# A two-layer state-space network on one core: the second layer's tail in chunks, its gating on GpSimd, and another choice of transposed products

## The chip, the cores and the metric

The kernel runs on one core of one Trainium2 chip. The metric is device time in microseconds (us) of one launch. Engines are named as in the profile: PE is TensorE (PEld its weight loads), DVE is VectorE, ACT is ScalarE, POOL is GpSimd, SP is SyncE, which here only issues DMAs. "PSUM" is the memory that PE writes to; it has 8 banks of 512 columns.

## The reference, cut to what matters

Input x is 16 images of 48 x 48 positions (L = 2304) with 96 channels. Two layers follow each other, and each is a residual state-space block and then a residual quantised feed-forward block:

```
for layer in (0, 1):
    n  = layernorm_over_channels(x)                 # no scale, no bias
    xc, z = split(n @ in_proj_w.T)                  # 192 + 192 channels
    u  = silu(depthwise3x3(xc) + conv_b)
    for k in 4 directions (rows, columns, both reversed):
        dt, B, C = u_k @ x_proj_w[k].T              # 6 + 16 + 16
        delta = softplus(dt @ dt_proj_w[k].T + b)
        h[t] = exp(delta[t]*A) * h[t-1] + delta[t]*u[t]*B[t]   # 192 channels x 16 states
        y_k[t] = sum over 16 states of h[t]*C[t]
    y  = sum of the four y_k, put back in row order, + Ds*u
    layer 0:  y = y*silu(z);  x = x + y @ out_w.T + (conv branch of y, with a squeeze gate)
    layer 1:  y = (y - mean_c y) / sqrt(var_c y + 1e-5) * g + b
              x = x + (y*silu(z)) @ out_w.T
    x = x + quantised_ffn(layernorm(x))             # 96 -> 384 -> 96, float8 and float16 rounding
```

## The kernel before, in words

The 16 images of layer 0 run first, then the 16 of layer 1 (`images`: a hardware loop over 15 images and a last pass of its own). Work is channels on partitions, positions along the free axis. The 192 channels of two directions are packed in three tiles: j = 0 holds channels 0 to 127 of one direction, j = 2 the same of its partner, j = 1 the remaining 64 channels of both. Positions are cut in NC = 3 chunks of CH = 768.

**The scan.** A *block* (`g` in the code, 0 to 17) is one tile and one chunk: ORDER = (1, 2, 0), so blocks 0 to 5 are tile 1, 6 to 11 tile 2, 12 to 17 tile 0. Of each tile's six blocks the first three (p = 0) are directions that run forwards, the other three (p = 1) backwards. A block has 16 *steps* (n), one for each state. In a step ACT makes exp(delta*A) (line 1167), PE brings B to all partitions, DVE does the recurrence as one TENSOR_TENSOR_SCAN over 768 positions (line 1486), POOL multiplies by C (line 1630), which SP has fetched with a DMA, and PE adds the result to a sum in PSUM (`add_state`, line 813) four steps later (LAG = 4). Up to six state buffers (NW) and four of h*C (NH) lie between the engines.

B comes in one of two ways. In a *plain* step PE broadcasts B by two bf16 matmuls (line 801) and DVE multiplies delta*u by it (line 1481) before the scan. In a *turned* step ACT scales the transposed delta*u by B (line 1233, `scale_du`) and PE transposes the product into PSUM (line 781, `turn_product`), so DVE does the scan alone. `TURNED` lists the turned steps by tile, `TURNED_FIRST` those of block 0. Other work is hung on steps by `STEP_AT`: the next block's delta (POOL lines 1649 to 1663, ACT 1133 to 1153), its transposition on PE at step 15 (line 773), z of the input projection in blocks 2 to 5 (line 707), the merge of tile 1's column order in blocks 7 to 9 at step 8 (lines 717, 718), and in `add_state`, for p = 1 blocks, the sums so far and D*u (lines 818, 819, with step 12), and for tile 0 the column-order sum (line 823, with step 14).

**The second layer's tail** (`norm` on PE, ACT and DVE) follows block 17. y lies in `yg` (128 + 64 channels). In order: ACT moves the last chunk's sum out of PSUM (`move_sums`, line 1267) and turns z into silu(z) (`gates`, 1255); PE takes the mean over channels by matmuls with 1/192 (`means`, 1012 and 1014), DVE subtracts it (1572), ACT squares (1318), PE takes the mean of the squares; PE also multiplies silu(z) by the bias part of the weight (`out_proj`, 1021 and 1023: the "shift"); DVE multiplies y by silu(z) (1578); PE projects that; ACT takes the square root (1327), DVE the reciprocal (1584), and DVE scales the projection by it (1590) and adds the shift (1593). PE transposes back to positions on partitions (1030) and DVE adds the residual (1598). All of it is done in two halves of 1152 positions, in PSUM units of 3 banks that are claimed in turn (`claim`, `released`). Between these lie the next image's layer norm on DVE and ACT (`ln_center`, `ln_spread`, `ln_apply`, lines 516 to 541) and its transposition on PE (666).

**The feed-forward part and the front.** The ffn follows in the tail of both layers; next to it DVE and PE do the next image's 3x3 convolution (DVE lines 569 and 572, PE line 691 by diagonal matmuls in four strips), and ACT copies its input (`fill_pad`). ACT then applies silu: `planes` (lines 1091, 1092) to PE's strips, and in `front` line 1060 gives `u[0]`, in row order, and 1061 gives `u[2]`, in column order. Everything of the next image's x_proj (PE 653) waits for them.

Of the kernel before, what the change touches and what calls it, by code (L numbers as in the profile page):

```python
# [82 lines left out]
TURNED = {0: (2, 4, 6, 9, 10, 13, 14, 15), 1: (4, 6, 10, 13, 14), 2: (2, 4, 6, 9, 10, 13, 14, 15)}  # L83
# [52 lines left out]
def columns(layer):  # L136
# [17 lines left out]
    "x_kept": 16, "unit_full": (26, 22),  # L154
# [10 lines left out]
    "z_ready": len(Z_UNITS), "z_copied": len(Z_UNITS), "sz_ready": 2, "merge_ready": NC, "merge_taken": NC, "gated": (0, 4),  # L165
# [3 lines left out]
    "mu_taken": (0, 4), "y_squared": (0, 4), "shift_kept": (0, 2), "ysd_kept": (0, 2), "yrstd_ready": (0, 2), "o_scaled": (0, 2), "o_shifted": (0, 2), "x1_ready": 2,  # L169
# [10 lines left out]
def metaformer(nc, x, wpacks, consts_f, consts_b, mid, c_rows, out):  # L180
    ctx = ExitStack()
    with ctx:
# [398 lines left out]
        U_MU, U_SHIFT, U_VAR, U_SHIFT_1, U_OUT, U_OUT_T = 2, 4, 5, 7, 8, 10  # L581
        U_Q = (16, 12)
# [3 lines left out]
        def _(pe):  # L586
# [8 lines left out]
            def released(k):  # L595
# [13 lines left out]
                for first, end, name, n in [  # L609
                        (U_MU, U_SHIFT, "mu_taken", 2), (U_SHIFT, U_VAR, "shift_kept", 1), (U_VAR, U_SHIFT_1, "ysd_kept", 1),  # L610
                        (U_SHIFT_1, U_OUT, "shift_kept", 2),
                        (U_OUT, U_OUT_T, "o_scaled", 1), (U_OUT_T, q, "x1_ready", 1)]:
                    if first <= k < end:
                        return name, n * (k - first + 1)
# [217 lines left out]
            def scan(g):  # L832
                for n in range(NS):
# [25 lines left out]
            def last_sums():  # L859
                for it in range(NIT - LAG, NIT):  # L860
                    add_state(it)

            def tail(layer, more):
                emptied(NG - 1)
                if layer == 0:
                    branch(more)
                else:
                    norm(more)
# [933 lines left out]
```

## Time and profile before

| | |
|---|---|
| runs shown (3) | 26275.84, 26275.85, 26290.46 us; median 26275.85 |
| profiled execution | 26276.13 us, span 26274.3 us |
| busy: PE, DVE | 24252.3 us (92%), 24337.4 us (93%) |
| busy: ACT, POOL | 22766.6 us (87%), 20551.8 us (78%) |
| granted TensorE clock | 0.981 of full speed |
| DMA queue q1 | 3762.72 MB, 46.0% of 16 engines' span |

Busy time is the union of an engine's instructions. Four engines are all above 75%, so the shares alone don't tell which of them a stage waits for: that is read from the idle time in front of an instruction and what ended it.

### The profile page before, as it was taken

To read this page: it belongs to the slowest core of one execution; us is meant where nothing else is said; L and a number is where in the kernel's file an instruction comes from. 1 tells how busy PE (TensorE), PEld (TensorE's weight loads), DVE (VectorE), ACT (ScalarE), POOL (GpSimd) and SP (SyncE) were. 2 spreads that over 40 slices of the span, in tenths; PEclk is the share of its full clock that TensorE was granted. 3 is DMA by queue.
4 is the path that set the end of the run, shared out by engine and by line. 5 is a ranking of instruction groups with operands and counts; after the bars stand their busy time and mean duration, and the time that the engine had idled before them with its cause. 6 is when DMAs were issued, how large, how long until landed. Compare 5 with 4: busy or idle time off the path is not lost.

```text
span 26274.3 us, 387148 instructions
## 1 busy us (share of the span) xinstructions
PE 24252.3 (92%) x96864; PEld 13557.9 (52%) x96864; DVE 24337.4 (93%) x17193; ACT 22766.6 (87%) x52523; POOL 20551.8 (78%) x11796
## 2 busy tenths in 40 slices
PE   8999999999999999999989999999999999999998
PEld 4555555555555555555545555555555555555555
DVE  8999999999999999999989999999999999999999
ACT  8888988889888988889878898888998888988888
POOL 7777977788777977779767887777987777977778
PEclk9999999999999999999999999999999999999999
DMA  4444544445444544445444554444544444544444
GB/s 155 132 134 132 170 133 133 134 144 158 132 134 133 163 140 132 136 133 169 129 124 142 157 160 143 145 144 143 164 151 143 145 143 142 172 143 144 144 143 148
DMA packets 1419236, 3790.06 MB, mean 144 GB/s; under 512 B 205888, under 2 KB 206016, under 8 KB 1416384
## 3 DMA queue, kind: packets, MB, share of 16 engines
q1 hardware_dynamic: 1416768, 3762.72, 46.0%
q8 instruction: 870, 14.25, 0.2%
q14 instruction: 1598, 13.09, 0.2%
HBM read 3686.39 MB, written 47.19 MB: 142 GB/s over the span
## 4 chain that ended last, share of the span: by engine, by line
PE 15%; issue 13%; DVE 12%; ACT 8%; POOL 2%; DMA 1%; DVEq 0%; ACTq 0%; SPq 0%; POOLq 0%
PE ps L813 6%; DVE arena L1486 5%; DVE ps L1481 5%; ACT arena L1233 3%; PE ps L781 2%; ACT arena L1167 2%; POOL arena L1630 1%; PE ps L691 1%; PE ps L801 1%; PE ps L653 1%; PE ps L818 1%; PE ps L819 1%; DMA arena<-c_rows 1%; PE ps L638 1%; PE ps L823 1%
## 5 line engine op out<-in xcount | busy, mean ns | idle before, releaser
L1630 POOL TENSOR_TENSOR arena<-arena 128x768 f32<-128x768 f32 x9216 | 16572.7, 1825 | 1456.8 <-DVE arena L1486 1157.4
L813 PE MATMUL ps<-arena,consts 128*128 128x384 f32 x36864 | 13643.2, 493 | 239.5 <-ACT arena L1267 189.1
L1486 DVE TENSOR_TENSOR_SCAN arena<-arena,carry,ps 128x768 f32<-128x768 f32 x6144 | 10910.5, 1805 | 428.6 <-PE ps L781 259.2
L1167 ACT ACTIVATE arena<-arena,An 128x768 f32<-128x768 f32 x9216 | 8448.1, 930 | 549.4 <-POOL arena L1630 538.1
L813 PEld LDWEIGHTS ps<-arena,consts 128*128 128x128 f32 x36864 | 6316.9, 191 | 3962.8 <-issue 458.6
L1486 DVE TENSOR_TENSOR_SCAN arena<-arena,ps 128x768 f32<-128x768 f32 x3072 | 5287.5, 1746 | 400.5 <-PE ps L781 293.6
L1481 DVE TENSOR_TENSOR ps<-ps,arena 128x768 f32<-128x768 f32 x5216 | 4921.2, 943 | 304.4 <-PE ps L801 299.7
L1233 ACT ACTIVATE arena<-arena 128x64 f32<-128x64 f32 (+1 forms) x14976 | 4266.3, 367 | 457.1 <-PE ps L781 436.0
L781 PE MATMUL ps<-consts,arena 128*128 128x128 f32 x24000 | 3384.7, 277 | 989.3 <-DVE arena L1486 769.0
L1233 ACT ACTIVATE arena<-arena,bT 128x64 f32<-128x64 f32 (+1 forms) x14592 | 4170.0, 368 | 96.8 <-PE ps L781 75.9
L781 PEld LDWEIGHTS ps<-consts,arena 128*128 128x128 f32 x24000 | 2752.8, 142 | 2815.3 <-issue 1591.9
L801 PE MATMUL ps<-arena,consts_b 96*128 96x512 bf16 x10432 | 2619.0, 333 | 374.3 <-DVE arena L1486 338.0
L801 PEld LDWEIGHTS ps<-arena,consts_b 96*128 96x128 bf16 x10432 | 896.2, 98 | 2600.2 <-DVE arena L1486 1363.0
L1644 POOL TENSOR_TENSOR arena<-arena 64x1152 bf16<-64x1152 f32 x32 | 75.8, 2368 | 2191.2 <-ACT arena L1122 2123.3
L572 DVE SCALAR_TENSOR_TENSOR arena<-arena,wp 128x2304 f32<-128x2304 f32 (+1 forms) x896 | 1731.7, 1933 | 29.4
L1667 POOL MEMSET arena<- 128x100 f32 x112 | 21.2, 189 | 1996.8 <-DVE arena L1561 1089.2
L1244 ACT COPY carry<-arena 128x1 f32<-128x1 f32 x6144 | 1084.0, 176 | 0.2
L1654 POOL TENSOR_TENSOR arena<-arena 128x768 f32<-128x768 f32 x544 | 992.7, 1825 | 0.0
L1663 POOL TENSOR_TENSOR arena<-arena 128x768 f32<-128x768 f32 x544 | 992.2, 1824 | 0.0
L1658 POOL TENSOR_TENSOR arena<-arena 128x768 f32<-128x768 f32 x544 | 990.8, 1821 | 0.0
L1649 POOL TENSOR_TENSOR arena<-arena 128x768 f32<-128x768 f32 x544 | 989.5, 1819 | 0.0
L740 PE MATMUL ps<-arena,wp 12*128 12x384 f32 x2304 | 934.2, 526 | 18.3 <-ACT bT L1178 18.3
(183 smaller groups left out, 19135.0 us busy)
## 6 DMA issues: line engine op xcount, KB each, us to landing
arena<-c_rows SPq DMA_DIRECT2D x6144, 384.0 KB, 3.8
arena<-c_rows SPq DMA_DIRECT2D x6144, 192.0 KB, 3.6
arena<-x SPq DMA_DIRECT2D x32, 864.0 KB, 7.2
arena<-arena SPq DMA_DIRECT2D x384, 72.0 KB, 2.7
arena<-mid SPq DMA_DIRECT2D x32, 864.0 KB, 6.7
c_rows<-arena SPq DMA_DIRECT2D x96, 192.0 KB, 3.2
mid<-arena SPq DMA_DIRECT2D x16, 864.0 KB, 3.9
out<-arena SPq DMA_DIRECT2D x16, 864.0 KB, 3.9
```

Source lines behind the costliest of these rows:

```text
L572: i = dve.scalar_tensor_tensor(out=o, in0=src, scalar=w[:, tap:tap + 1], in1=o, op0=ALU.mult, op1=ALU.add)
L781: mm = pe.transpose(slots[it % 2][:, i * P:(i + 1) * P], prod[turned_before(it) % 2][:, i * P:(i + 1) * P], ident)
L801: mm = pe.matmul(slots[it % 2][:, a:a + m], sel[:, at:at + P], stacks[p][0:96, c * CH + a:c * CH + a + m], start=True, stop=True)
L813: mm = pe.matmul(y_part[:, h, :], ident, hC[it % NH][:, h * SEG:(h + 1) * SEG], start=(n == 0), stop=(n == NS - 1))
L1167: act.activation(state_at[it % NW], delta[g % 2], ACT.Exp, scale=An[:, slot(s) * NS + n:slot(s) * NS + n + 1]).then_inc(sem["da_ready"], 1)
L1233: last = act.activation(prod[q % 2][:, at], duT[g % 2][:, at], ACT.Copy, scale=bT[p][:, TBL * c + i, n, h:h + 1])
L1244: act.copy(carry[:, n:n + 1], state_at[it % NW][:, end:end + 1]).then_inc(sem["end_kept"], 1)
L1481: dve.tensor_tensor(slots[it % 2], slots[it % 2], du[g % 2], ALU.mult).then_inc(sem["dbu_ready"], 1)
L1486: dve.tensor_tensor_scan(a[:, ::back], a[:, ::back], slots[it % 2][:, ::back], 0.0 if k == 0 else carry[:, n:n + 1], ALU.mult, ALU.add).th ...
L1630: pool.tensor_tensor(hC[it % NH], state_at[it % NW], Csb[b], ALU.mult).then_inc(sem["hc_ready"], 1)
L1654: pool.tensor_tensor(e, spln, e, ALU.add).then_inc(sem["sp_log1p"], 1)
L1663: pool.tensor_tensor(du[g % 2], delta[g % 2], chunk(u[j], c), ALU.mult).then_inc(sem["du_ready"], 1)
```

## The change

Three edits. `TURNED` changes: tiles 0 and 2 turn step 13 no longer (7 turned steps instead of 8), tile 1 turns steps 3, 4, 9, 13, 15 instead of 4, 6, 10, 13, 14. The second layer's tail works by chunks of 768 in the order 1, 2, 0 (`DONE`; block 17 is chunk 0): the mean of chunk 1 is taken in block 17 at step 8 and that of chunk 2 between the last four sums; ACT's `gates` and the first squares run before the last chunk's sum is moved; POOL multiplies y by silu(z); fixed PSUM places (`done_part`) stand in for the claimed units. In the tail's ffn and in the front, ACT's order changes: `planes(1, 0)` goes between the third and fourth relu, `planes(1, 1)` and `u[0]` (`u_of_rows`) go before the second copy of y16, `planes(0, 2)` moves into `front`.

```diff
-TURNED = {0: (2, 4, 6, 9, 10, 13, 14, 15), 1: (4, 6, 10, 13, 14), 2: (2, 4, 6, 9, 10, 13, 14, 15)}
+TURNED = {0: (2, 4, 6, 9, 10, 14, 15), 1: (3, 4, 9, 13, 15), 2: (2, 4, 6, 9, 10, 14, 15)}
...
+        def done_part(q, rows):
+            return ps[0:rows, DONE_AT[q]:DONE_AT[q] + 2 * BANK].rearrange("p (g x) -> p g x", x=BANK)[:, :, 0:SEG]
...
+        DONE = (1, 2, 0)
+        DONE_AT = (0, 4 * BANK, 2 * BANK)
...
@@ PE
+                    if At.layer == 1 and g == NG - 1 and n == STEP_AT["second"]:
+                        means_ahead(1)
...
             def last_sums():
                 for it in range(NIT - LAG, NIT):
+                    if At.layer == 1 and it == NIT - 2:
+                        means_ahead(2)
                     add_state(it)
...
             def norm(more):
+                means(0, done_part(2, P)).then_inc(sem["unit_full"], 1)
+                for q, c in enumerate(DONE):
+                    pe.wait_ge(sem["y_squared"], v("y_squared", 2 * q + 2))
+                    pe.wait_ge(sem["mu_taken"], v("mu_taken", (0, 4, 6)[q]))
+                    over_channels(done_part(q, DM), (mean_w[:, 0:DM], mean_w[0:DB, 0:DM]), ysq, c).then_inc(sem["unit_full"], 1)
                 pe.wait_ge(sem["sz_ready"], v("sz_ready", 2))
+                for q, c in enumerate(DONE):
+                    pe.wait_ge(sem["ysd_kept"], v("ysd_kept", q + 1))
+                    over_channels(done_part(q, DM), (wgb[:, 1, 0, :], wgb[0:DB, 1, 1, :]), sz, c).then_inc(sem["unit_full"], 1)
+                for q, c in enumerate(DONE):
                     if more:
+                        transpose_x(1, (range(2), range(2, 4), range(4, 5))[q])
+                    pe.wait_ge(sem["shift_kept"], v("shift_kept", q + 1))
+                    pe.wait_ge(sem["gated"], v("gated", 2 * q + 2))
+                    over_channels(done_part(q, DM), (wgb[:, 0, 0, :], wgb[0:DB, 0, 1, :]), yg, c).then_inc(sem["unit_full"], 1)
...
+            def over_channels(to, w, src, c):
+
+                for t, m in ((0, P), (1, DB)):
+                    for h in range(2):
+                        at = c * CH + h * SEG
+                        mm = pe.matmul(to[:, h, :], w[t], src[t][0:m, at:at + SEG], start=(t == 0), stop=(t == 1), skip_group_check=True)
+                return mm
+
+            def means_ahead(c):
+
+                if c == 1:
+                    pe.wait_ge(sem["y_moved"], v("y_moved", NG - 1))
+                    pe.wait_ge(sem["merge_taken"], v("merge_taken", NC))
+                    pe.wait_ge(sem["duT_ready"], v("duT_ready", NG))
+                else:
+                    pe.wait_ge(sem["scanned"], v("scanned", NIT - 1))
+                means(c, pre_part if c == 1 else done_part(1, P)).then_inc(sem["mu_full"], 1)
...
@@ ACT
             def front(layer):
...
-                planes(0, 3)
+                for g in (2, 3):
+                    planes(0, g)
...
+            def u_of_rows(at):
+
+                act.wait_ge(sem["conv_tap"], v("conv_tap", 18 * at + 9))
+                act.activation(u[0], conv, ACT.Silu, bias=wcol("conv_b")[:, 0:1]).then_inc(sem["u_ready"], 1)
...
                 for n in range(6) if more else ():
                     act.wait_ge(sem["f_q16"], v("f_q16", n + 1))
                     act.activation(f16[n], f16[n], ACT.Relu, bias=b1q[:, n % 3:n % 3 + 1]).then_inc(sem["f_b16"], 1)
-                if more:
-                    planes(1, 0)
+                    if n == 2:
+                        planes(1, 0)
...
-                    if more:
-                        planes(1, h + 1)
+                    if more and h == 0:
+                        planes(1, 1)
+                        u_of_rows(1)
 
             def norm(more):
                 gates()
+                squares(0)
+                move_sums(NG - 1)
+                squares(1)
+                if more:
+                    ln_square(act, "in", ALL, at=1)
+                squares(2)
                 nc.scalar.preload_act_table_set("sqrt_and_others")
...
@@ DVE
             def norm(more):
+                for q in range(2):
+                    dve.wait_ge(sem["mu_full"], v("mu_full", q + 1))
+                    less_mean(q, (pre_part, done_part(1, P))[q])
+                dve.wait_ge(sem["hc_ready"], v("hc_ready", NIT))
                 if more:
                     ln_center(dve, "in", xin, ALL, lambda c: dve.wait_ge(sem["x_loaded"], v("x_loaded", 32)), at=1)
...
+                full(U_MU)
+                less_mean(2, done_part(2, P))
                 if more:
                     ln_spread(dve, "in", EPS_IN, 0, ALL[0], at=1)
-                dve.wait_ge(sem["sz_ready"], v("sz_ready", 2))
-                dve.wait_ge(sem["y_squared"], v("y_squared", 4))
-                for t in range(2):
-                    dve.tensor_tensor(yg[t], yg[t], sz[t][0:(P, DB)[t], :], ALU.mult).then_inc(sem["gated"], 2)
-                if more:
                     ln_apply(dve, "in", xc, 0, ALL[0], at=1)
...
@@ POOL
+                else:
+                    pool.wait_ge(sem["sz_ready"], v("sz_ready", 2))
+                    for q, c in enumerate(DONE):
+                        for t, m in ((0, P), (1, DB)):
+                            pool.wait_ge(sem["y_squared"], v("y_squared", 2 * q + t + 1))
+                            pool.tensor_tensor(chunk(yg[t], c), chunk(yg[t], c), chunk(sz[t][0:m, :], c), ALU.mult).then_inc(sem["gated"], 1)
```

The reciprocals, the scaling and the shift on DVE (lines 1584 to 1593) and ACT's square roots and copies become three chunks each in the same way. `more` is false for the last image of a layer alone.

## Rows read from the trace of the kernel before

**Rows 1.** The page's first line.

```profile
span 26274.3 us, 387148 instructions
```

**Rows 2.** Busy time in stretches of a second-layer image: blocks 1, 5, 6, 17, tail.

```profile
core 0: us, PE busy (x) PEld busy (x) DVE busy (x) ACT busy (x) POOL busy (x), PEclk, DMA share, GB/s
...
14412.05:14452.15 40.10, 37.45 (x157) 19.68 (x156) 38.12 (x28) 37.14 (x103) 36.15 (x21) 1.00 0.56 165
...
14567.96:14606.31 38.35, 35.72 (x139) 19.06 (x139) 37.97 (x29) 35.28 (x90) 35.72 (x21) 1.00 0.54 166
14606.31:14640.63 34.32, 30.68 (x133) 17.70 (x133) 34.05 (x24) 32.64 (x80) 32.97 (x20) 1.00 0.57 172
...
15012.30:15051.31 39.01, 35.86 (x144) 20.22 (x143) 35.42 (x24) 26.87 (x66) 29.62 (x17) 1.00 0.49 156
15051.31:15167.82 116.51, 105.68 (x400) 57.14 (x399) 97.43 (x74) 76.36 (x74) 2.41 (x5) 0.93 0.05 14
```

**Rows 3.** The same view of a first-layer image: block 6, with the gates.

```profile
4526.38:4567.52 41.14, 33.67 (x135) 19.96 (x135) 34.37 (x24) 40.59 (x86) 37.54 (x22) 0.92 0.52 170
```

**Rows 4.** The page's groups of instructions for the scan.

```profile
L1630 POOL TENSOR_TENSOR arena<-arena 128x768 f32<-128x768 f32 x9216 | 16572.7, 1825 | 1456.8 <-DVE arena L1486 1157.4
...
L1481 DVE TENSOR_TENSOR ps<-ps,arena 128x768 f32<-128x768 f32 x5216 | 4921.2, 943 | 304.4 <-PE ps L801 299.7
```

**Rows 5.** Timeline, end of block 11: start, us, engine, idle before.

```profile
14820.44 0.82 PE L781 MATMUL ps<-consts,arena 128*128 128x128 f32 x6
14821.10 1.46 PE L813 MATMUL ps<-arena,consts 128*128 128x384 f32 x4
14822.39 0.82 PE L781 MATMUL ps<-consts,arena 128*128 128x128 f32 x6
...
14827.47 0.97 DVE L1481 TENSOR_TENSOR ps<-ps,arena 128x768 f32<-128x768 f32 x1 [0.46 <-PE ps L801]
```

**Rows 6.** Timeline, first step of block 13.

```profile
14861.15 1.56 PE L813 MATMUL ps<-arena,consts 128*128 128x384 f32 x4 [0.58 <-POOL arena L1630]
...
14863.07 0.97 DVE L1481 TENSOR_TENSOR ps<-ps,arena 128x768 f32<-128x768 f32 x1 [1.18 <-PE ps L801]
```

**Rows 7.** Timeline, step 8 of block 1.

```profile
14433.40 0.97 DVE L1481 TENSOR_TENSOR ps<-ps,arena 128x768 f32<-128x768 f32 x1 [1.08 <-PE ps L801]
```

**Rows 8.** Timeline, end of block 17 and the second layer's tail.

```profile
14255.53 6.62 PE L813 MATMUL ps<-arena,consts 128*128 128x384 f32 x20
14255.73 1.81 DVE L1486 TENSOR_TENSOR_SCAN arena<-arena,carry,ps 128x768 f32<-128x768 f32 x1 [2.71 <-PE ps L781]
...
14259.56 1.95 DVE L516 TENSOR_REDUCE small<-arena 128x18 f32<-128x1728 f32 x1 [2.02 <-POOL arena L1630]
...
14262.18 0.80 ACT L1267 COPY arena<-ps 128x768 f32<-128x768 f32 x1 [10.23 <-PE ps L813]
...
14263.03 2.20 PE L1012 MATMUL ps<-arena,consts 128*128 128x384 f32 x6 [0.89 <-ACT arena L1267]
...
14267.40 2.61 DVE L1572 TENSOR_TENSOR arena<-arena,ps 128x1152 f32<-128x1152 f32 x2 [3.69 <-PE ps L1014]
...
14276.34 5.02 DVE L1578 TENSOR_TENSOR arena<-arena 128x2304 f32<-128x2304 f32 x2
...
14283.57 14.55 DVE L1584 RECIPROCAL arena<-arena 96x1152 f32<-96x1152 f32 x2
...
14302.02 1.35 DVE L1593 TENSOR_TENSOR arena<-arena 96x1152 f32<-96x1152 f32 x1
14303.43 3.15 PE L1030 MATMUL ps<-consts,arena 96*128 96x96 f32 x18 [4.52 <-DVE arena L1593]
```

**Rows 9.** Timeline, ffn and front: ACT's wait, silu of rows; a convolution tap.

```profile
14341.42 2.61 DVE L572 SCALAR_TENSOR_TENSOR arena<-arena,wp 128x2304 f32<-128x2304 f32 x1
...
14344.78 0.56 ACT L1307 CAST arena<-ps 128x480 f16<-128x480 f32 x1 [4.81 <-PE ps L904]
...
14347.52 2.22 ACT L1060 ACTIVATE arena<-arena,wp 128x2304 f32<-128x2304 f32 x1 [0.26 <-issue]
```

More of the change, by code:

```diff
@@ L608, in released @@
                     return ("br_scaled", k - U_BR + 1) if k < U_BR_T else ("x1_ready", k - U_BR_T + 1)
[L609 to L614, printed above, removed]
+                return "x1_ready", k - U_OUT_T + 1
             def front(layer):
@@ L1017, in out_proj, with means @@
-            def out_proj(k, src, q, h):
-                claim(k)
-                for g in range(3):
-                    pe.matmul(segs(k, (0, DM))[:, g, :], wgb[:, q, 0, :], in_order(src[0], h, g), start=True, stop=False)
-                for g in range(3):
-                    mm = pe.matmul(segs(k, (0, DM))[:, g, :], wgb[0:DB, q, 1, :], in_order(src[1][0:DB, :], h, g), start=False, stop=True)
-                mm.then_inc(sem["unit_full"], 1)
+            def means(c, to):
+                return over_channels(to, (mean_w, mean_w[0:DB, :]), yg, c)
@@ L1026, in to_tokens @@
             def to_tokens(k, src, h):
-                claim(k)
+                if At.layer == 0:
+                    claim(k)
                 for i in range(9):
@@ L1508, in tail @@
                     gate_sums()
-                else:
-                    dve.wait_ge(sem["hc_ready"], v("hc_ready", NIT))
-                if layer == 0:
                     branch(more)
@@ L1534, in tail, with less_mean @@
                 i.then_inc(sem["o_ready"], 1)
+            def less_mean(q, mean):
+                for t, m in ((0, P), (1, DB)):
+                    o = halves(chunk(yg[t], DONE[q]))
+                    dve.tensor_tensor(o, o, mean[0:m, :, :], ALU.subtract).then_inc(sem["mu_taken"], 1)
             def rounded(n):
@@ new lines, in norm @@
+                for q, c in enumerate(DONE):
+                    dve.wait_ge(sem["ysd_kept"], v("ysd_kept", q + 1))
+                    dve.reciprocal(chunk(yrstd_T, c), chunk(yrstd_T, c)).then_inc(sem["yrstd_ready"], 1)
+                for q, c in enumerate(DONE):
+                    o = chunk(out_T, c)
+                    dve.wait_ge(sem["yrstd_ready"], v("yrstd_ready", q + 1))
+                    full(U_OUT + q)
+                    dve.tensor_tensor(halves(o), done_part(q, DM), halves(chunk(yrstd_T, c)), ALU.mult).then_inc(sem["o_scaled"], 1)
+                    dve.wait_ge(sem["o_scaled"], v("o_scaled", q + 1))
+                    dve.wait_ge(sem["shift_kept"], v("shift_kept", q + 1))
+                    dve.tensor_tensor(o, o, chunk(shift_T, c), ALU.add).then_inc(sem["o_shifted"], 1)
```

86 lines of the change are left out of this document (22 added, 64 removed).

## The prediction

> **What bounds the kernel now.** I read the page first: the span is 26274.3 us [rows 1], and by the table above four engines are 78 to 93% busy, so no share settles anything. Then the busy time in stretches cut at the end of each block's last scan. A second-layer image takes 795 us: 680 in 18 blocks and 116.51 in the tail, ffn and front [rows 2]. In most blocks DVE is the engine without slack: in block 5 it is busy 37.97 of 38.35 us. In block 17 it is busy 35.42 of 39.01 and something else sets the pace [rows 2]. The timeline shows what. The last scan of block 17 waited 2.71 us for PE's transposition, and PE ran on without a pause after it, with the five sums still owed to it [rows 8]. Blocks 15 and 16 show the same wait. At the end of block 11 (10 is alike) DVE waits 0.46 us at the next block's first step, PE again running through [rows 5]. At the start of block 13 the chain is longer: PE waits for POOL, and DVE then 1.18 us for PE [rows 6]. A POOL multiplication is 1825 ns [rows 4] and a block needs 16 of them plus 4 for delta: up to 36.5 us (they overlap a little) against block lengths of 34.3 to 39. So DVE binds tile 1, DVE, POOL and PE are nearly level in tiles 2 and 0, and PE binds blocks 15 to 17. In the tail two engines are late together: DVE's reciprocals end at 14298.12 and PE's last projection at 14298.55 by the timeline, and the way back to tokens starts at 14303.43 [rows 8].
>
> **Part 1, turned steps of tiles 2 and 0 (12 blocks of an image).** Step 13 becomes plain. DVE gets one multiplication more, 943 ns [rows 4], 0.97 us with its gap. PE replaces six transpositions by two broadcasts: a transposed product holds PE for 14821.10 - 14820.44 = 0.66 us [rows 5], a broadcast for 0.33 in the same timeline, so 0.33 less. ACT loses six scalings, 1.85 us together. What 0.97 costs depends on the waits that it fills.
> - Blocks 15 to 17 (both layers): PE sets the end; DVE's 0.97 goes into the 2.71 us wait [rows 8], and 0.33 comes back: -1.0 for three.
> - Blocks 9, 10, 11: three turned steps in a row behind the sums of p = 1. PE needs 0.66 + (14822.39 - 14821.10 = 1.29) = 1.95 us for one [rows 5] and DVE 1.74, hence waits of about 0.21 each and 0.46 after them [rows 5]. They go, and with them what the plain step costs: 0, and -0.1 for block 9.
> - Blocks 12 to 14: the next block starts with a wait of 1.18 [rows 6], then 0.54 and 0.5: DVE is too fast for POOL. It gives 2.3 back of 2.9: +0.65.
> - Blocks 6 to 8, second layer: block 6 has no wait at all (34.05 busy of 34.32 [rows 2]), but block 7 opens with one like rows 6, so 0.97 returns; blocks 8 and 9 open with 0.2 only: +1.5.
> - Block 6, first layer: ACT binds, 40.59 of 41.14 us [rows 3], because of the gates. The 1.85 us that it loses shorten the block; part comes back as the POOL wait of block 7: -1.3. Blocks 7 and 8 pay in full, +1.9.
>
> Sum: second layer +1.05 an image, first layer +0.2; over 16 images of each together +20 us. The ends: nothing filled is 12 x 0.97 x 32 = +372; everything filled and PE's share back is -0.33 x 12 x 32 = -127. I take the middle value because the waits were counted block by block.
>
> **Part 2, turned steps of tile 1.** Five stay five; ACT needs 12 scalings (2.96 us) for each. Block 1 loses its stall: it takes 40.10 us against 38.35 of block 5 [rows 2], because PE, busy with a turned step 6 and the C rows of steps 6 and 7, comes 1.08 us late at step 8 [rows 7] and some 0.5 at step 7. With step 6 plain, DVE takes 0.97 more there and PE 0.33 less: -1.4. The C rows fall in blocks 0 and 1 alone, and block 0 keeps TURNED_FIRST. Block 3 has a second wait behind steps 13 and 14: -0.2. Steps 3 and 4 in a row ask ACT for 2 x 2.96 us at a point where it runs some four steps ahead: 0. Sum -1.6 x 32 = -51 us; bounds 0 (stall stays) and -2.0 an image.
>
> **Part 3, the means ahead in block 17.** A mean of one chunk is four matmuls of 384; six in the old form took 2.13 us a tile (14263.03 to the next line's start 14265.16), so a chunk takes 2/3 of 4.26 = 2.84 us [rows 8]. It goes in at step 8, in front of turned steps 9 and 10, and behind it everything of block 17 that PE does is late, its transpositions for DVE above all. PE has 1.5 us idle there before steps 9 and 10; from step 12 on it has none (the 2.71 us wait shows it). So block 17 gets 2.84 - 1.5 = +1.3 us longer, x 16 = +21. Bounds: 0 and 2.84.
>
> **Part 4, the tail.** T is the end of the last scan, 14257.54. Before: sums end T+4.6, moved T+5.4, PE starts at 14263.03, T+5.5; DVE waits 3.69 for the first mean; gating 5.02; the transposition back starts at T+45.9 [rows 8]. After, with pieces of 768 (DVE 0.94 with PSUM in, ACT 0.80, four matmuls 2.84):
> - PE: the sums owed run from T-2.0 at 6.62 / 5 = 1.32 each [rows 8]; the mean of chunk 2 goes between the third and the fourth, so they end at T+7.5, not 4.6, and ACT has moved them at T+8.3. This is the price: queued behind that mean are the last two sums, and behind them the last mean.
> - Mean of chunk 0 to T+11.2. DVE subtracts chunk 1 at T+0.1 and chunk 2 at T+5.0, centres the next image T+6.9 to 11.1 (4.15 us from 14259.56 [rows 8]), subtracts chunk 0 to T+13.2.
> - PE then has nine products of 2.84 and 2.6 us of transpositions in a row: variances to T+19.7, shifts to T+28.2, projections to T+39.3. The waits inside hold: squares of the last chunk T+14.4 against a need at 16.9; square roots T+16.8, 17.8, 20.7 against 19.7, 22.5, 25.3.
> - POOL gates: six of 1825 ns [rows 4], 10.9 us from T+2, the last at about T+18; needed from T+29. DVE's 5.02 us [rows 8] vanish at no cost as long as POOL has these 11 us in hand.
> - DVE: spread and apply to T+18.3, reciprocals 14.55 us [rows 8] to T+32.9. So DVE, which was level with PE, is no longer last; the last projection is. It is scaled and shifted in 0.93 + 0.95 (2/3 of 1.29 and 1.35 + gap): T+41.2 against T+45.9.
>
> -4.6 us an image, x 16 = -74. Bounds: -1.8 (PE waits once for each product) and -7.5 (PE's start is not late).
>
> **A rule against it.** DVE and POOL run side by side in the whole scan at one duration, POOL 1825 ns and DVE 943 [rows 4], but there DVE's second input comes from PSUM. The Trainium skill ("SBUF — State Buffer", Who interferes with whom) says that a DVE instruction with two SBUF inputs and a GpSimd instruction that reads SBUF block each other. No row here shows such a pair. What it would do is a rival below.
>
> **Part 5, ACT's order in ffn and front.** ACT stands idle 4.81 us for the second ffn product while silu of u[0] is still owed [rows 9]. It could start once the last tap of the first tile ends, 14341.42 + 2.61 = 14344.03 [rows 9]. From then on ACT has the same 13 us of work as before from 14344.78, without the 0.26 us gap [rows 9]: the last silu ends 0.75 + 0.26 = 1.0 us earlier, and x_proj, which waits for it, too. PE's third strip starts 0.7 earlier; the relus that planes(1, 0) pushes back by 2.8 end at 14337.4, DVE asks from 14339.4; the copy of y16 is 1.5 later and DVE takes it 7 us after. The first layer shows a 4.80 us wait in the same place. -1.0 x 30 images = -30; bounds 0 and -60.
>
> **Sum.** +20 - 51 + 21 - 74 - 30 = -114 us. From the profiled 26276.13: 26162; that run lies 0.3 above the median of the three shown. I say 26160.
>
> **Rivals.**
> - *The waits do not give back* (slower). 12 blocks x 0.97 x 32 = +372 in place of +20: 26276 + 372 - 51 + 21 - 74 - 30 = 26514. For it: tile 1's blocks show DVE at 37.97 of 38.35. Against: the waits of rows 5, 6, 8. It decides once DVE's added time exceeds the waits from step 13 to the next block's step 0; the sum turns positive when more than 134 us of the 372 stay beyond what I count. Chance 0.10.
> - *The tail is PE's alone*: the means put ahead cost all 2.84 and the chunk waits halve the gain: +20 - 51 + 45 - 32 - 30 = -48, 26228. For it: PE was busy from 14263.03 to 14298.55. Chance 0.18.
> - *More comes back*: fewer scalings on ACT and a less hurried POOL remove all waits after step 13 (-1.5 an image in place of +0.6), the early mean costs 0.6, and the tail gains 6: -48 - 51 + 10 - 96 - 30 = -215, 26061. For it: ACT is busy 37.14 of 40.10 us in block 1 and 35.28 of 38.35 in block 5 [rows 2]. Chance 0.17.
> - *POOL's gates block DVE's two-input steps*: the subtraction and the product of the next image's norm, 1.96 us each, each wait up to one gate, 1.8 us. Reciprocals end at T+36.5, then three pairs of 1.88: T+42.1 in place of 41.2, +0.9 x 16 = +14: 26176. This is what the rule of the Trainium skill would make. Chance 0.10.
> - The forecast as it stands: 0.45.
>
> **Range and chances.** 26050 to 26275 leaves out most of the slow rival and the far end of the fast one. A change of under 0.2% (53 us) can't be told from none by this measurement. Faster by over 0.2% (below 26223): forecast, port rival, fast rival, little of the second: 0.72. Within 0.2%: 0.17. Slower: 0.11.
>
> **What would show it.** Right: blocks 15 and 16 shorter by 0.3; block 1 near 38.8; blocks 7, 8, 13, 14 within 1 us of before, and no wait of DVE at their first step; block 17 near 40; transposition back at T+41; reciprocals ended 6 us before the last projection; ACT's wait before y16 gone and x_proj's last part 1 us earlier. Wrong: blocks 6 to 14 all near 36.4 plus unchanged waits; reciprocals late behind the square roots; PE idle between the nine products; PE's added mean pushing the last scan by 3 us.

## The result, and the profile after

The changed kernel takes 26115.58 us, the median of 5 runs (26108.82 to 26116.4), against 26276.27 of the kernel before (median of 5 on the same chip). The ratio is 0.9938, 95% interval 0.9924 to 0.9952: 161 us faster, where 116 were forecast (26160 us). One of the five executions of the kernel before took 58796.38 us; the median of the other four is 26276.06, so it changes nothing. The profiled execution took 26116.4 us. The page of the kernel after, its span, busy times and the scan's groups (line, engine, operation, count | busy us, mean ns | idle before, releaser):

```profile
span 26114.6 us, 381945 instructions
...
PE 24103.6 (92%) x95328; PEld 13330.2 (51%) x95328; DVE 24585.9 (94%) x17625; ACT 22109.2 (85%) x50283; POOL 20746.8 (79%) x11892
...
L1646 POOL TENSOR_TENSOR arena<-arena 128x768 f32<-128x768 f32 x9216 | 16574.4, 1825 | 1406.1 <-DVE arena L1506 1090.0
...
L1501 DVE TENSOR_TENSOR ps<-ps,arena 128x768 f32<-128x768 f32 x5600 | 5281.6, 943 | 160.0 <-PE ps L801 157.0
```

The durations are those of before; DVE has 384 products more, one for each of 12 blocks in 32 images, and its waits in front of them fell from 304.4 to 160.0 us [rows 4]. DVE works 248 us more than before in a span that is 160 us shorter: the gain is in waits. The busy time in stretches, first block 6 of a first-layer image (the answer to rows 3), then of a second-layer image blocks 1, 5, 6, 15, 17 and the tail (the answer to rows 2; columns as there):

```profile
4511.42:4551.33 39.91, 33.30 (x131) 19.61 (x130) 35.13 (x25) 38.70 (x80) 37.46 (x22) 0.91 0.53 177
...
14352.92:14391.86 38.94, 36.64 (x157) 19.77 (x156) 38.02 (x28) 36.82 (x104) 35.94 (x21) 1.00 0.57 169
14506.43:14544.72 38.29, 35.23 (x140) 19.19 (x139) 37.91 (x29) 34.85 (x90) 35.74 (x21) 1.00 0.58 167
14544.72:14580.04 35.32, 31.45 (x133) 17.61 (x131) 35.01 (x25) 31.96 (x76) 33.95 (x21) 1.00 0.54 169
14875.17:14912.69 37.52, 35.88 (x145) 20.41 (x144) 35.13 (x25) 32.82 (x79) 37.13 (x22) 1.00 0.56 176
14951.44:14991.14 39.70, 38.08 (x148) 21.24 (x147) 36.52 (x27) 30.44 (x63) 30.05 (x17) 1.00 0.51 153
14991.14:15101.34 110.20, 102.97 (x393) 54.81 (x391) 94.45 (x77) 72.12 (x76) 14.44 (x11) 0.95 0.05 15
```

Block 6, which had no wait, is 1.0 us longer; block 1 is 1.2 shorter, the tail 6.3. Cut in the same way and averaged over the 16 images of a layer (tail and front over 15: behind the sixteenth something else follows), in us (the blocks not named changed by less than 0.2):

| block | layer 0, before, after | layer 1, before, after | part |
|---|---|---|---|
| 0 | 39.75, 39.81 | 39.75, 40.08 | |
| 1 | 40.14, 38.97 | 40.14, 38.97 | 2 |
| 3 | 39.45, 38.22 | 39.27, 38.02 | 2 |
| 4 | 38.39, 38.59 | 38.49, 38.56 | 2 |
| 6 | 40.84, 39.18 | 34.38, 35.36 | 1 |
| 7, 8 | 76.38, 78.41 | 75.62, 76.38 | 1 |
| 9 | 37.65, 38.08 | 37.91, 37.72 | 1 |
| 12, 13, 14 | 107.59, 108.36 | 107.57, 108.35 | 1 |
| 15 | 38.78, 37.55 | 38.76, 37.55 | 1 |
| 16 | 39.10, 38.77 | 39.10, 38.77 | 1 |
| 17 | 39.04, 38.71 | 39.04, 39.71 | 1, 3 |
| tail and front | 152.3, 151.5 | 116.0, 110.0 | 4, 5 |

The first layer's tail and front differ by up to 2 us from image to image (151.0 to 153.1 before, 150.1 to 152.8 after), so its 0.8 us is no firm figure.

The tail of the first second-layer image of the kernel after, with the end of block 17 (timeline: start, us, engine, line, operation, idle before). Its last scan ends at T = 14200.80 + 1.81 = 14202.61:

```profile
14200.80 1.81 DVE L1506 TENSOR_TENSOR_SCAN arena<-arena,carry,ps 128x768 f32<-128x768 f32 x1 [1.95 <-PE ps L781]
...
14204.48 2.94 PE L1021 MATMUL ps<-arena,consts 128*128 128x384 f32 x8
14207.34 2.85 PE L813 MATMUL ps<-arena,consts 128*128 128x384 f32 x8
14210.23 0.80 ACT L1280 COPY arena<-ps 128x768 f32<-128x768 f32 x1 [5.03 <-PE ps L813]
14211.08 11.80 PE L1021 MATMUL ps<-arena,consts 128*128 128x384 f32 x32 [0.89 <-ACT arena L1280]
14211.37 1.96 DVE L522 TENSOR_TENSOR arena<-arena,small 128x1728 f32<-128x1728 f32 x1
14211.85 8.46 POOL L1704 TENSOR_TENSOR arena<-arena 128x768 f32<-128x768 f32 x4 [3.79 <-ACT arena L1350]
14214.16 1.81 DVE L1557 TENSOR_TENSOR arena<-arena,ps 128x768 f32<-128x768 f32 x2 [0.83 <-PE ps L1021]
14215.89 1.94 DVE L532 TENSOR_REDUCE small<-arena 128x18 f32<-128x1728 f32 x1
14217.86 0.72 DVE L534 TENSOR_SCALAR small<-small 128x18 f32<-128x18 f32 x1
...
14218.87 0.27 DVE L538 RECIPROCAL small<-small 128x18 f32<-128x18 f32 x1 [0.28 <-ACT small L555]
...
14219.28 2.85 DVE L541 TENSOR_TENSOR arena<-arena,small 128x1728 f32<-128x1728 f32 x1
14222.05 14.56 DVE L1601 RECIPROCAL arena<-arena 96x768 f32<-96x768 f32 x3
...
14239.18 0.95 DVE L1606 TENSOR_TENSOR arena<-ps,arena 96x768 f32<-96x768 f32 x1 [0.77 <-PE ps L1021]
14239.34 2.91 PE L1021 MATMUL ps<-arena,wgb 128*96 128x384 f32 x8
...
14242.28 0.95 DVE L1606 TENSOR_TENSOR arena<-ps,arena 96x768 f32<-96x768 f32 x1 [1.16 <-PE ps L1021]
14243.27 0.95 DVE L1609 TENSOR_TENSOR arena<-arena 96x768 f32<-96x768 f32 x1
14244.28 3.15 PE L1039 MATMUL ps<-consts,arena 96*128 96x96 f32 x18 [2.04 <-DVE arena L1609]
```

PE's last sum ends at 14210.19, T+7.6; it waits 0.89 for the copy and from 14211.08 it runs without a wait to its last projection, which ends at 14242.25, T+39.6. The reciprocals end at 14236.61, T+34.0, so DVE stands idle 1.16 us for that projection. The way back to tokens starts at T+41.7, against T+45.9 [rows 8].

The front of the same image, ACT alone:

```profile
14280.29 0.92 ACT L1105 ACTIVATE arena<-ps,wp 64x384 f32<-64x384 f32 x1
14285.13 2.22 ACT L1094 ACTIVATE arena<-arena,wp 128x2304 f32<-128x2304 f32 x1 [3.91 <-DVE arena L572]
14287.37 0.56 ACT L1320 CAST arena<-ps 128x480 f16<-128x480 f32 x1
```

ACT now waits for the last tap and applies silu at once; the copy of y16 stands behind it without a wait of its own, where it had waited 4.81 [rows 9].

### The profile page after: what moved, and what is told of

Read it like the earlier page. It is cut to its first block, busy times and chain, and to the rows that moved or that the text cites. A ratio compares the mean times of both kernels' runs of the same rounds, so it can differ in the third digit from the quotient of the medians.

```text
span 26114.6 us, 381945 instructions
## 1 busy us (share of the span) xinstructions
PE 24103.6 (92%) x95328; PEld 13330.2 (51%) x95328; DVE 24585.9 (94%) x17625; ACT 22109.2 (85%) x50283; POOL 20746.8 (79%) x11892
## 4 chain that ended last, share of the span: by engine, by line
PE 29%; DVE 26%; issue 25%; ACT 13%; POOL 4%; DMA 2%; DVEq 1%; SPq 0%; ACTq 0%; POOLq 0%
DVE arena L1506 11%; PE ps L813 11%; DVE ps L1501 10%; ACT arena L1246 5%; POOL arena L1646 3%; ACT arena L1180 3%; DVE arena L572 3%; PE ps L691 3%; PE ps L781 3%; PE ps L1021 2%; DMA arena<-c_rows 2%; PE ps L801 2%; PE ps L653 1%; PE ps L638 1%; PE ps L823 1%
## 5 line engine op out<-in xcount | busy, mean ns | idle before, releaser
L1501 DVE TENSOR_TENSOR ps<-ps,arena 128x768 f32<-128x768 f32 x5600 | 5281.6, 943 | 160.0 <-PE ps L801 157.0
L781 PE MATMUL ps<-consts,arena 128*128 128x128 f32 x21696 | 3055.8, 277 | 946.3 <-DVE arena L1506 750.0
L1246 ACT ACTIVATE arena<-arena 128x64 f32<-128x64 f32 (+1 forms) x13824 | 3907.9, 365 | 20.3
L1246 ACT ACTIVATE arena<-arena,bT 128x64 f32<-128x64 f32 (+1 forms) x13440 | 3813.8, 367 | 20.4
L781 PEld LDWEIGHTS ps<-consts,arena 128*128 128x128 f32 x21696 | 2482.8, 141 | 2613.2 <-issue 1425.6
L801 PE MATMUL ps<-arena,consts_b 96*128 96x512 bf16 x11200 | 2809.8, 332 | 529.7 <-DVE arena L1506 487.2
L801 PEld LDWEIGHTS ps<-arena,consts_b 96*128 96x128 bf16 x11200 | 950.5, 98 | 2949.2 <-DVE arena L1506 1648.6
```

The lines of the kernel that those rows point to most:

```text
L781: mm = pe.transpose(slots[it % 2][:, i * P:(i + 1) * P], prod[turned_before(it) % 2][:, i * P:(i + 1) * P], ident)
L801: mm = pe.matmul(slots[it % 2][:, a:a + m], sel[:, at:at + P], stacks[p][0:96, c * CH + a:c * CH + a + m], start=True, stop=True)
L1246: last = act.activation(prod[q % 2][:, at], duT[g % 2][:, at], ACT.Copy, scale=bT[p][:, TBL * c + i, n, h:h + 1])
L1501: dve.tensor_tensor(slots[it % 2], slots[it % 2], du[g % 2], ALU.mult).then_inc(sem["dbu_ready"], 1)
```

## The experiments

The first four kernels hold parts of the change alone; the others are the changed kernel with one thing altered. Times are medians; the kernel before had 26274.57 us beside e1 to e4, 26271.81 beside e5 to e8 and 26276.31 beside e9 and e10, which ran on another chip than the eight. The ratios are to these. The changed kernel was not run again beside them, so a difference to its 26115.58 us carries some 5 us that can't be told apart. Nor is one stretch equally long where its code is the same: from the first transposition back to tokens to the next image's first scan, second-layer images average 70.1, 69.7 and 69.6 us in the profiled executions of the kernel before, e1 and e2, and 68.4, 68.9 and 69.0 in those of the changed kernel, e5 and e7. Half a microsecond there is 8 us in 16 images, so for small differences the rows up to the tokens say more than the whole.

**The parts.** e1 and e2 are the kernel before with one edit of its lists:

```diff
# e1
-TURNED = {0: (2, 4, 6, 9, 10, 13, 14, 15), 1: (4, 6, 10, 13, 14), 2: (2, 4, 6, 9, 10, 13, 14, 15)}
+TURNED = {0: (2, 4, 6, 9, 10, 14, 15), 1: (4, 6, 10, 13, 14), 2: (2, 4, 6, 9, 10, 14, 15)}
# e2
+TURNED = {0: (2, 4, 6, 9, 10, 13, 14, 15), 1: (3, 4, 9, 13, 15), 2: (2, 4, 6, 9, 10, 13, 14, 15)}
```

> The kernel before with the new turned steps of tiles 2 and 0 alone (step 13 plain in 12 blocks of each image). Theory (the plain step's 0.97 us on DVE fills waits for PE and POOL): block by block the changed kernel shows +1.0 in blocks 6 (second layer), 7 and 8, +0.4 in 12 and 14, -1.2 in 15, -0.3 in 16 and 17, -1.7 in the first layer's block 6: together -0.5 us an image in layer 0 and +0.4 in layer 1, so 26274 us, no change. Rival (DVE bound, nothing filled): 12 x 0.97 x 32 = +372, 26648. Rival (the gain of the whole change comes mostly from here, by fewer scalings on ACT): -100, 26176.

> The kernel before with the new turned steps of tile 1 alone (3, 4, 9, 13, 15 for 4, 6, 10, 13, 14). Theory: PE is relieved where the C rows and the second z product make it late, blocks 1 and 3 each 1.2 us shorter, block 4 0.1 to 0.2 longer, all else the same: -2.1 x 32 = -67, 26209 us. Rival (blocks 1 and 3 gain only what the blocks after them give back, POOL being nearly level): under -20, above 26256.

e3 is the kernel before with ACT's order in ffn and front alone (u_of_rows and the places of `planes`, as in the change); e4 is the changed kernel with `TURNED` of before, so tail, means ahead and ACT's order together.

> The kernel before with ACT's new order in ffn and front alone (planes(1,0) after the third relu, planes(1,1) and u[0] before the second copy of y16, planes(0,2) in the front). Theory: the silu chain starts at DVE's last tap of the first tile and not at the second ffn product, 0.9 us earlier in 30 images: -27, 26249 us. Rival (x_proj waits for PE, whose third strip is the limit): 0, 26276. Rival (the next image's norm or ffn is pushed back): +30.

> The changed kernel with the turned steps of before: tail by chunks with gating on GpSimd, and ACT's order. Theory (the parts add up): 26116 + 69 = 26185 us, block 17 of the second layer 1.0 us longer than before and the rest of the scan as before. Rival (the early mean in block 17 costs all of its 2.84 us where three turned steps stand in a row): 26214.

| | measured us (range) | ratio, 95% interval | against before | forecast of the parts |
|---|---|---|---|---|
| e1 | 26268.87 (26259.1 to 26281.25) | 0.9998, 0.9989 to 1.0008 | -6 | +20 (part 1) |
| e2 | 26193.35 (26173.74 to 26205.85) | 0.9969, 0.9957 to 0.998 | -81 | -51 (part 2) |
| e3 | 26248.12 (26240.4 to 26254.98) | 0.999, 0.998 to 0.9999 | -26 | -30 (part 5) |
| e4 | 26190.71 (26177.7 to 26200.42) | 0.9969, 0.9957 to 0.998 | -84 | -83 (parts 3, 4, 5) |

-6 - 81 - 84 = -171, against -161 measured for the whole: the parts are nearly independent. e4 less e3 is -57 for tail and means. In e4 block 17 of the second layer takes 40.04 us, 39.04 before; that is the early mean's +1.0, 16 us in all, and leaves -73 for the tail. By the rows the tokens start at T+41.7 in place of T+45.9 in every one of 15 images: -4.2 us, or -67 in 16. The two parts on which the forecast erred are the lists.

**Who gates (e5).** The six products y * silu(z) go to DVE, behind the next image's `ln_spread`:

```diff
@@ DVE, norm
+                dve.wait_ge(sem["sz_ready"], v("sz_ready", 2))
+                for q, c in enumerate(DONE):
+                    for t, m in ((0, P), (1, DB)):
+                        dve.wait_ge(sem["y_squared"], v("y_squared", 2 * q + t + 1))
+                        dve.tensor_tensor(chunk(yg[t], c), chunk(yg[t], c), chunk(sz[t][0:m, :], c), ALU.mult).then_inc(sem["gated"], 1)
@@ POOL: the same six products, taken out
```

> The changed kernel, but DVE does the six gate multiplications, behind its spread. Theory (in the tail PE's nine products set the end, and DVE has 5.4 us in hand before the last projection): six times 0.87 us less the 1.4 us that POOL now blocks DVE: reciprocals end at T+37.6 instead of 33.8, then three pairs, of which the last ends at about T+43.5 instead of 41.7: +1.8 x 16 = +29, 26145 us. Rival (gating on GpSimd is what brings the tail's gain): +5.2 x 16 = +83, 26199. Rival (fully hidden): 26116.

Measured: 26134.06 us (26131.0 to 26136.17), ratio 0.9946 (0.993 to 0.9963), 18 us slower than the changed kernel. DVE in the tail of e5; its last scan ends at T = 14196.72:

```profile
14211.97 0.18 DVE L534 TENSOR_SCALAR small<-small 128x18 f32<-128x18 f32 x1
14212.08 5.29 DVE L1602 TENSOR_TENSOR arena<-arena 128x768 f32<-128x768 f32 x6
...
14217.70 1.96 DVE L541 TENSOR_TENSOR arena<-arena,small 128x1728 f32<-128x1728 f32 x1 [0.15 <-DVE small L538]
14219.58 14.56 DVE L1607 RECIPROCAL arena<-arena 96x768 f32<-96x768 f32 x3
```

The gates cost DVE 5.29 us, but the reciprocals end only 3.4 us later, at T+37.4 in place of T+34.0: without POOL beside it, L534 is back from 0.72 to 0.18 and L541 from 2.85 to 1.96, 1.43 us less. From T+37.4 the three pairs of scale and shift follow without a wait, and tokens start at T+43.0. So gating on POOL is worth 1.3 us an image, 21 us, against 18 measured in the whole; most of the tail's gain is not from it.

**When the means are taken.** In e6 the mean of chunk 1 is taken with that of chunk 2, between the last sums, and no longer in block 17:

```diff
@@ PE, block 17
-                    if At.layer == 1 and g == NG - 1 and n == STEP_AT["second"]:
-                        means_ahead(1)
@@ PE, last_sums
                     if At.layer == 1 and it == NIT - 2:
+                        means_ahead(1)
                         means_ahead(2)
```

> The changed kernel with the mean of chunk 1 taken between the last sums, beside that of chunk 2, and no longer in block 17. Theory (PE is without slack in both places): block 17 of the second layer 1.0 us shorter, the last sums and all behind them 2.84 us later: +1.8 x 16 = +29, 26145 us. Rival (the early mean buys nothing, since the last product is bound by DVE): -16, 26100.

Measured: 26153.82 us (26136.83 to 26155.85), ratio 0.9952 (0.9935 to 0.9969), 38 us slower than the changed kernel. Block 17 is 1.0 us shorter (38.71), and tokens start at T+44.6 in place of T+41.7. Taking 2.9 us of work ahead costs 1.0 where it lands and saves about 3.0 where it stood (3.5 if the whole tail and front is taken, which scatters). With e5's 1.3 that makes 4.3, as much as the 4.2 us by which the tokens moved up: by this sum, an estimate, all the rest (three chunks in place of two halves, and the mean of chunk 2 ahead of two sums, which e7 shows to be badly placed) comes to nothing. No run held both edits.

In e7 the mean of chunk 2 goes behind the last sum instead of ahead of two sums, and DVE centres the next image before it subtracts that mean:

```diff
@@ PE, last_sums
-                    if At.layer == 1 and it == NIT - 2:
-                        means_ahead(2)
                     add_state(it)
+                if At.layer == 1:
+                    means_ahead(2)
```

> The changed kernel with the mean of chunk 2 behind the last sum instead of in front of the last two, and DVE centring the next image before it subtracts that mean. Theory (PE sets the tail's end and stood idle 0.9 us for ACT to move the last sum, which the mean now fills): -0.9 x 16 = -14, 26102 us. Rival (the squares of chunk 2 and the centring come later and PE waits for them): +1 to +3 us an image, 26132 to 26164.

Measured: 26104.42 us (26101.35 to 26107.73), ratio 0.9936 (0.9919 to 0.9952), 11 us faster than the changed kernel, or 7 if each is taken from the kernel before beside it, too little to be sure of by the time alone. The rows are clearer. PE at the end of block 17 and in the tail of e7, then DVE and POOL in its tail:

```profile
14193.46 6.62 PE L813 MATMUL ps<-arena,consts 128*128 128x384 f32 x20
14199.91 14.66 PE L1021 MATMUL ps<-arena,consts 128*128 128x384 f32 x40
```

```profile
14199.49 1.46 DVE L519 TENSOR_SCALAR small<-small 128x18 f32<-128x18 f32 x1
...
14210.91 2.84 DVE L541 TENSOR_TENSOR arena<-arena,small 128x1728 f32<-128x1728 f32 x1 [0.15 <-DVE small L538]
...
14197.33 3.58 POOL L1705 TENSOR_TENSOR arena<-arena 128x768 f32<-128x768 f32 x2
14204.80 7.14 POOL L1705 TENSOR_TENSOR arena<-arena 128x768 f32<-128x768 f32 x4 [3.88 <-ACT arena L1350]
```

The 0.89 us in which PE waited for ACT's copy is filled by that mean, and tokens start at T+40.5 (T = 14195.47) in all 15 images, 1.2 us earlier. The forecast's price, two sums and the last mean queued behind the mean of chunk 2, was real, and this order avoids it.

**PE's sums at the end of a block (e8).** In p = 1 blocks eight matmuls for the sums so far and D*u fall together at n = 8 of `add_state`, which is reached in step 12, and in tile 0 four more at n = 10, in step 14. e8 halves and spreads them:

```diff
+SUMS_AT, COLUMNS_AT = (1, 7), (3, 8)
...
-                if p == 1 and n == 8:
-                    for h in range(2):
+                if p == 1 and n in SUMS_AT:
+                    h = SUMS_AT.index(n)
...
-                if p == 1 and j == 0 and n == 10:
-                    for h in range(2):
+                if p == 1 and j == 0 and n in COLUMNS_AT:
+                    h = COLUMNS_AT.index(n)
```

> The changed kernel with add_state's extra matmuls (sums so far, D*u, column order) spread over plain steps: half 0 of the first pair with state 1, half 1 with state 7, the column sums with states 3 and 8. Theory (blocks 15 to 17 are longer than 36.4 us only because these 5.2 us of PE fall on steps 12 and 14, behind which turned steps stand; PE has 1.1 us to spare in each plain step before): blocks 15, 16, 17 shorter by 1.0, 2.0, 1.5 to 2.0: -4.7 x 32 = -150, 25966 us. Rival (PE is bound over the whole block): under -30, above 26086. Rival (POOL, 35.6 us a block, takes over at once): -50 to -100.

Measured: 25975.32 us (25964.26 to 25984.91), ratio 0.9885 (0.9868 to 0.9901), 140 us faster than the changed kernel. Blocks 15 and 16 of a second-layer image of e8, busy time as in rows 2:

```profile
14794.92:14830.88 35.96, 35.73 (x147) 21.00 (x146) 35.34 (x25) 32.91 (x80) 35.45 (x21) 1.00 0.54 174
14830.88:14867.71 36.83, 36.34 (x148) 21.13 (x148) 36.30 (x27) 33.72 (x85) 35.95 (x21) 1.00 0.55 175
```

Block 15 falls from 37.5 to 36.0 us with PE as busy as before (35.88 to 35.73), block 16 from 38.8 to 36.8 and block 17 of the first layer from 38.7 to 36.4: there was no lack of PE time in these blocks, the work only stood in the wrong place, ahead of the transposition that DVE needed. Block 17 of the second layer, which also holds the mean, fell only from 39.7 to 39.2. Block 9 is longer by 1.4 us in layer 0 and 0.9 in layer 1, since a half of its sums now stands ahead of the merge.

**Behind the merge (e9).** In blocks 7 to 9 DVE waits for PE at the first turned step behind the merge.

```diff
+TURNED_MERGE = (2, 4, 6, 10, 12, 14, 15)
...
-    return it % NS in (TURNED[group(g)[2]] if g > 0 else TURNED_FIRST)
+    return it % NS in (TURNED_MERGE if 7 <= g <= 9 else TURNED[group(g)[2]] if g > 0 else TURNED_FIRST)
```

> The changed kernel with one thing altered: in blocks 7, 8 and 9, where the chunks' sums are merged, the turned steps are 2, 4, 6, 10, 12, 14 and 15 instead of those of the tile's list, so that each of the steps behind the merge is no longer two turned ones close together. Theory (in these blocks PE is early enough and the waits behind a merge are for DVE's turned products to be read): the waits behind the merge fall from 1.68 to about 0.9 us a block, 0.85 x 3 blocks x 32 images = 82 us: 26034 us. Rival (what is taken from these waits comes back at the next step, as PE or POOL is then last): within 15 us of the changed kernel, 26100 to 26130 us. Second rival (more untouched steps there load PE): 26150 us or more.

Measured: 26072.74 us (26059.58 to 26074.28), ratio 0.992 (0.9904 to 0.9937), 43 us faster than the changed kernel and half of what was expected. The step behind the merge in block 8, first in the changed kernel, then in e9:

```profile
14641.09 3.76 DVE L1506 TENSOR_TENSOR_SCAN arena<-arena,carry,ps 128x768 f32<-128x768 f32 x2 [1.33 <-PE ps L781]
```

```profile
14604.58 0.97 DVE L1502 TENSOR_TENSOR ps<-ps,arena 128x768 f32<-128x768 f32 x1 [1.00 <-PE ps L802]
```

With a plain step in that place the wait is 1.00 in place of 1.33, and the 0.2 behind it are gone: 0.57 a block in 7 and 8 in both layers, 0.34 in block 9 of layer 0, nothing in block 9 of layer 1. The theory holds for a third of the wait; what is left I take to be the merge's own matmuls on PE, which was not tried.

**All together (e10).** e7's order, the spread sums (7 and 8 in block 9), the list of e9 also in block 17, and `TURNED_FIRST` = (4, 10, 13, 14).

> The changed kernel with the edits that the runs so far point to, together: the state sums in blocks 15 to 17, 3 and 9 spread (7 and 8 in block 9, so that no half of a sum stands ahead of the merge), the mean of chunk 2 put behind the last sums, the list of the merging blocks for 7, 8, 9 and 17, and steps 4, 10, 13 and 14 turned in the first block of a stretch. Theory (each part is worth what it was alone): 26116 - 140 (spread sums) - 11 (mean) - 82 (merge list) - 37 - 24 - 42 (block 9, block 17 and the first block) = 25780 us. Rival (the engines are within 2% of their sums, so the parts meet the same floor and give back half of what is new): 25870 us. If it is above 25975 us, the added lists cost more than they give.

Measured: 25892.79 us (25876.22 to 25894.71), ratio 0.9854 (0.9837 to 0.987). It beats both kernels: 223 us below the changed one, but 113 above the 25780 that were expected. With e9 as measured and nothing for the last two edits the sum is 26116 - 140 - 11 - 43 - 37 = 25885 (37 for block 9's loss in e8, (1.4 + 0.9) x 16), so the parts add up. The other two edits, for which 24 and 42 us were expected, brought next to nothing: block 0 takes 39.50 and 40.06 us against 39.81 and 40.08, and block 17 is 0.7 longer in layer 0 than in e8 (37.18, 36.44). Block 17 of a second-layer image in e10, then rows of PE and of DVE in it:

```profile
14805.81:14845.07 39.26, 37.77 (x146) 21.33 (x145) 36.39 (x27) 30.19 (x61) 31.27 (x18) 1.00 0.50 163
```

```profile
14824.35 2.94 PE L1024 MATMUL ps<-arena,consts 128*128 128x384 f32 x8
14827.21 1.56 PE L815 MATMUL ps<-arena,consts 128*128 128x384 f32 x4
14828.61 0.49 PE L803 MATMUL ps<-arena,consts_b 96*128 96x512 bf16 x2
```

```profile
14829.14 0.97 DVE L1504 TENSOR_TENSOR ps<-ps,arena 128x768 f32<-128x768 f32 x1 [1.77 <-PE ps L803]
```

Neither PE (37.77 of 39.26 us) nor DVE (36.39) is full there. DVE's longest wait, 1.77 us, is for the broadcast that PE makes only after the early mean (L1024) and a sum: here too the order counts, and no other place for the mean was tried.

## Why the prediction was right, and where its steps were off

The likeliest case happened, with 44 us more gain than forecast. By its steps:

- **Part 1, forecast +20, measured -6 (e1).** The waits gave back what was counted, block by block: blocks 6 to 14 were forecast at +2.05 for a second-layer image and came to +2.3; in the first layer +1.15 was forecast and +1.4 came. The step that failed is blocks 15 to 17, "-1.0 for three": they gave -1.9, and all of the difference is block 15, -1.2 instead of -0.3; 0.9 x 32 = 29 us, against 26 missing. DVE at the two ends of block 15 in the kernel before, and in the one after:

```profile
14935.02 0.97 DVE L1481 TENSOR_TENSOR ps<-ps,arena 128x768 f32<-128x768 f32 x1 [0.57 <-PE ps L801]
...
14971.47 1.75 DVE L1486 TENSOR_TENSOR_SCAN arena<-arena,ps 128x768 f32<-128x768 f32 x1 [2.78 <-PE ps L781]
```

```profile
14871.67 3.49 DVE L1506 TENSOR_TENSOR_SCAN arena<-arena,carry,ps 128x768 f32<-128x768 f32 x2
14875.09 0.95 DVE L1501 TENSOR_TENSOR ps<-ps,arena 128x768 f32<-128x768 f32 x1
...
14910.94 1.75 DVE L1506 TENSOR_TENSOR_SCAN arena<-arena,ps 128x768 f32<-128x768 f32 x1 [2.08 <-PE ps L781]
```

  Before, block 15 opened with a wait of 0.57; after, it opens with none. The forecast took PE as setting the end of all three blocks, so that only PE's 0.33 could come back. That holds for 16 and 17, which gave 0.33 each and still open with 0.5. But block 15 follows block 14, behind which PE is not late any more. The forecast had booked the opening waits of blocks 13, 14 and 15 as what 12 to 14 give back; block 12, though, pays with the one at its own opening [rows 5], 13 and 14 with theirs, and that of block 15 was left over. Of block 15's 1.2 us it is 0.6; another 0.35 lies between PE's products of steps 9 and 15 (16.95 us before, 16.60 after, the forecast 0.33), and some 0.3 ahead of step 9, which I did not resolve.
- **Part 2, forecast -51, measured -81 (e2).** Block 1 was forecast at -1.4 and gave -1.17; what is left is a wait at step 8. Block 3 was forecast at -0.2 and gave -1.2. DVE near the end of block 3, before and after:

```profile
14523.26 1.75 DVE L1486 TENSOR_TENSOR_SCAN arena<-arena,ps 128x768 f32<-128x768 f32 x1 [1.43 <-PE ps L781]
14525.21 1.75 DVE L1486 TENSOR_TENSOR_SCAN arena<-arena,ps 128x768 f32<-128x768 f32 x1 [0.19 <-PE ps L781]
```

```profile
14461.96 1.75 DVE L1506 TENSOR_TENSOR_SCAN arena<-arena,ps 128x768 f32<-128x768 f32 x1 [0.43 <-PE ps L781]
```

  Steps 13 and 14 were both turned, right behind the eight matmuls in step 12, and the first waited 1.43 us, the second 0.19. I counted the second and passed over the first. With step 14 plain DVE has 0.97 us more ahead of step 15, and the wait at 13 is down to 0.43. Why it fell by a full 1.0 with step 13 turned in both lists was not tried by itself; turned steps 9 and 3 in place of 10 and 6 are the other differences ahead of it. e8, which takes half of those matmuls away from that place, shortens block 3 further (37.65 and 37.81 us), so the load there is what is waited for (block 4 gives 0.2 to 0.4 of it back).
- **Part 3, forecast +21, measured +16.** Block 17 1.0 us longer (e4 against before, e6 against the changed kernel), for 1.3.
- **Part 4, forecast -74, measured -73 (e4 less e3, less part 3), -67 by the rows.** So close an agreement of the times is partly luck. The forecast tail, point by point: last sum T+7.5, seen T+7.6; last projection T+39.3, seen T+39.6; tokens T+41.2, seen T+41.7; no wait of PE between its nine products, as forecast. Reciprocals were forecast at T+32.9 and ended at T+34.0, still off the path.
- **Part 5, forecast -30, measured -26 (e3).** In the image shown, 53.84 us from the start of to-tokens to the table load behind the last silu, 54.70 before: 0.9, for 1.0. e3's interval (0.998 to 0.9999) reaches from 3 to 53 us of gain, so the size is not well known, and that it is a gain rests on the rows as much as on the time.

The two misses, 26 us in part 1 and 30 in part 2, point the same way and account for the 44 us by which the whole was off. Of the rivals, the waits do give back (e1's interval ends at 1.0008, +21 us, where +372 was the price; the forecast's threshold of 134 us is for all that stays of the 372, 114 beyond the 20 counted), and the tail was not PE's alone in the sense of halving the gain. The fast rival was right in its first half: more came back than I counted, but in block 15 and block 3. Its reason, fewer scalings on ACT and a less hurried POOL, was not tested by itself; block 3 keeps its number of scalings, so there it can't be the reason. The port rival had the mechanism right, one of its two places, and not the price. POOL's gates do hold up DVE, by 0.55 us at L534 and 0.89 at L541, the product of the norm; the subtraction, L522, started before the gate and was not held. But both waits stand ahead of the reciprocals, and these had room: DVE's waits for the second and third projection are 0.77 and 1.16 us, 1.9 together, and in e5 reciprocals that end 3.4 us later cost 1.3. The 1.43 us fit into that room, so no 0.9 us came of it at the end. The Trainium skill ("SBUF — State Buffer", Who interferes with whom) says that the shared pair of ports is an exclusive lock and that issue order decides who blocks. Both directions stand in the rows: in e7 L519 starts at 14199.49, inside a gate that runs to 14200.91, and ends at 14200.95; and in the changed kernel the four gates take 8.46 us beside L522, which started first and kept its 1.96, against 7.14 for the same four in e7.

## What to carry to other kernels

Cut the span by stages, and look in each for the wait that repeats; a wait behind a cluster of matmuls is a question of order before it is one of load. Spreading twelve small matmuls over four steps (140 us) brought nearly as much as the whole change. When a moved instruction fills a wait, ask also which later wait, in the next stage, closes with it: the two misses here were both waits that stood in the trace and were not counted. Work taken ahead of a serial tail pays if the place where it lands has idle time on that engine (1.0 us paid for 3.0 saved). And work moved to a third engine can hold up the engine that it was taken from: here by 1.43 us, which cost nothing because DVE had 1.9 us in hand.

## What was not expected of the hardware

A TENSOR_SCALAR over 18 numbers of 128 partitions, 0.17 us by itself, took 1.46 us in e7 and 0.72 in the changed kernel because a POOL multiplication of 1.82 us was running: this DVE instruction with one input in SBUF waits too, and its length then does not depend on its own size but on what is left of POOL's (in e7 it ends 0.04 us after the gate). Not every small one does: L538, a RECIPROCAL over the same 18 numbers, took 0.27 us inside the four gates of the changed kernel and 0.25 in e5, where none ran. The reduction L532 (1.94) and the subtractions with one input in PSUM (L1557, 1.81 for two) kept their durations beside the same gates. The Trainium skill ("SBUF — State Buffer", Who interferes with whom) counts tensor_scalar among the operations that can take both ports and leaves reductions out; the rows agree.
